# Second attention layer of a fused transformer kernel: from one token tile to pairs of token tiles, with every product but the keys' and values' as split fp32r products

## The reference

```python
sim = jnp.einsum('hid,hjd->hij', qh, kh) * SCALE          # 128 ** -0.5
mean = jnp.mean(sim, axis=-1, keepdims=True)
sim = (sim - mean) * ATTN_MATRIX_SCALE + mean             # 1.5
attn = jax.nn.softmax(sim, axis=-1)
out = jnp.einsum('hij,hjd->hid', attn, vh)                # then @ Wout + bout
```

## Time and profile before

| | us |
|---|---|
| median of 3 runs | 1071.01 (1070.51 to 1073.47) |
| span of the profiled execution | 1066.7 |
| PE busy in the span | 989.8 (93%) |
| DVE, POOL, ACT busy | 552.8, 429.3, 399.9 |
| experts end, L1's keys begin on PE | 637.0 |
| first output product of L1 starts | 697.08 |
| last output product of L1 starts | 951.72 |

### The profile page before, as it was taken

The page is one execution under the profiler, slowest core; times in us unless marked ns, Lnnn a source line. Parts: engine busy times, 40 slices in busy tenths (PEclk is TensorE's granted clock), DMA queues, the critical chain, the costliest instruction groups (busy, mean ns, idle before and its releaser), DMA issues.

```text
span 1066.7 us, 19273 instructions
## 1 busy us (share of the span) xinstructions
PE 989.8 (93%) x6204; PEld 809.6 (76%) x6205; DVE 552.8 (52%) x1349; ACT 399.9 (37%) x1340; POOL 429.3 (40%) x599
## 2 busy tenths in 40 slices
PE   5999999999997749999999998899999999999995
PEld 3599999999996625555555555899999999985662
DVE  7645454445544642222222226767676777653363
ACT  0255555554542202222222222444443434335442
POOL 5343334343332024433443336746565544331242
PEclk9999999999999569999999999999999999999887
DMA  9600000000000843111111114100000000000002
GB/s 298 248 2 1 1 0 1 2 2 1 0 1 1 308 141 98 40 48 40 39 41 47 39 34 135 42 11 20 10 20 10 21 1 2 2 1 1 1 1 79
DMA packets 29016, 47.71 MB, mean 45 GB/s; under 512 B 4493, under 2 KB 23105, under 8 KB 28705
## 3 DMA queue, kind: packets, MB, share of 16 engines
q1 hardware_dynamic: 25553, 37.68, 10.4%
q0 software_dynamic: 3408, 9.31, 3.2%
HBM read 37.68 MB, written 9.31 MB: 44 GB/s over the span
## 4 chain that ended last, share of the span: by engine, by line
PE 87%; DVE 7%; issue 2%; POOL 1%; DMA 1%; ACT 1%; POOLq 0%; SPq 0%; DVEq 0%; ACTq 0%
PE banks L428 16%; PE banks L1087 12%; PE banks L413 11%; PE banks L1126 7%; PE banks L420 6%; PE banks L399 6%; PE banks L390 6%; PE banks L391 5%; PE banks L392 5%; PE banks L340 2%; PE banks L1297 2%; PE banks L1112 2%; PE banks L1301 1%; PE banks L925 1%; DMA region_b<-xn_rows,token_now 1%
## 5 line engine op out<-in xcount | busy, mean ns | idle before, releaser
L859 POOL TENSOR_TENSOR region_a<-region_a,recip 128x512 f32<-128x512 f32 x128 | 133.2, 1041 | 294.9 <-DVE recip L648 294.7
L428 PE MATMUL banks<-region_a 128*128 128x128 f32 x1536 | 193.0, 275 | 1.9 <-DVE oT_low L668 1.7
L428 PEld LDWEIGHTS banks<-region_a 128*128 128x128 f32 x1536 | 181.8, 192 | 3.4 <-issue 2.6
L1087 PE MATMUL banks<-W,region_b 128*128 x312 | 149.6, 603 | 0.6 <-ACT region_b L1134 0.6
L413 PE MATMUL banks<-xT,region_b 128*128 128x128 f32 x1024 | 129.9, 282 | 3.2 <-DVE q_low L589 1.4
L773 ACT ACTIVATE region_a<-banks,negmax 128x154 f32<-128x154 f32 x256 | 96.0, 388 | 90.8 <-DVE negmax L632 88.3
L413 PEld LDWEIGHTS banks<-xT,region_b 128*128 128x128 f32 x1024 | 124.0, 198 | 4.5 <-DVE q_low L589 1.8
L1173 DVE TENSOR_TENSOR region_b<-banks,region_a 128x512 f32<-128x512 f32 x78 | 54.0, 692 | 114.8 <-PE banks L1087 114.8
L1221 POOL TENSOR_TENSOR region_b<-region_b 128x512 f32<-128x512 f32 x39 | 49.3, 1264 | 146.5 <-DVE region_b L1173 144.4
L773 ACT ACTIVATE region_a<-banks,bias 128x308 f32<-128x308 f32 x128 | 65.0, 513 | 110.9 <-DVE bias L644 110.9
L668 DVE TENSOR_TENSOR oT_low<-banks,oT_high 128x256 fp32r<-128x256 f32 x128 | 54.3, 424 | 91.5 <-ACT oT_high L764 91.5
(11 more groups left out here) (207 smaller groups left out, 1760.7 us busy)
## 6 DMA issues: line engine op xcount, KB each, us to landing
W<-in_L_ffn_W SPq DMA_DIRECT2D x1, 8192.0 KB, 27.4
y_slots<-region_b SPq DMA_DIRECT2D x39, 128.0 KB, 1.7
region_a<-in_L_ffn_b SPq DMA_DIRECT2D x1, 4096.0 KB, 18.7
region_a<-in_L_ffn_W SPq DMA_DIRECT2D x1, 4096.0 KB, 29.8
region_b<-in_L_xattn_Wq SPq DMA_DIRECT2D x2, 1024.0 KB, 8.3
xn_rows<-region_b SPq DMA_DIRECT2D x1, 2048.0 KB, 9.4
out<-x SPq DMA_DIRECT2D x4, 512.0 KB, 3.0
region_b<-in_L_xattn_Wk SPq DMA_DIRECT2D x2, 768.0 KB, 6.1
```

The lines of the kernel that those rows point to most:

```text
L428: mm = pe.matmul(o_ps[:, u * P:(u + 1) * P], V[:, b, 2 * g + u, i, :], probsT[:, g % 2, m * P:(m + 1) * P], start=(i == 0), stop=(i == 2))
L859: pool.tensor_tensor(whole, pr[:, :, 0:split], rc.broadcast_to([P, L.hs, split]), ALU.mult)
L1087: mm = pe.matmul(banks[:, 2 * r + part, :], xgT[:, r, k, :], w, start=(k == 0), stop=(k == DK - 1))
```

## The change

L1 gets functions of its own: `pe_pairs`, `dve_pairs`, `act_pairs` and `pool_pairs`. The unit is a pair of token tiles; a body has 8 steps n, of head group n // 2 and tile n % 2, and 4 groups. Layer 0, the experts and the coupling keep their work. The keys are multiplied with a context that is already shifted by a third of its mean, so the additional score column and the two small DVE operations go. In the loop:

- q, scores, PV and output are all split fp32r products: q 12 per group, scores 6 per step (308 columns), PV 18 per group, output 24 per tile; q and PV have 256 moving columns (both tiles). Weights and V are split ahead (`Wq_high`, `Wq_low`, `V_high`, `V_low`).
- Probabilities are normalised in place by one POOL instruction of 640 columns; ACT takes the high part of all 640 transposed columns, DVE the rest. Both happen in every step. High part and rest of q and o are of 512 columns, four times per pair each.
- In each step PE issues the transposes of the step before, and then the scores of the next one.

```diff
+                for n in range(8):
+                    s = 8 * i + n
+                    if not (first and n == 0):
+                        pe.wait_ge(sem("p_norm"), s0 + s)
+                        if not (first and n == 1):
+                            pe.wait_ge(sem("pt2_low"), s - 1)
+                        pe_pair_probsT(pe, (n - 1) % 8)
+                    if not (last and n == 7):
+                        if n % 2 == 1:
+                            pe.wait_ge(sem("q2_sb"), 4 * i + (n + 1) // 2 + 1)
+                        if not (first and n == 0):
+                            pe.wait_ge(sem("p_exp"), s0 + s)
+                        pe_pair_scores(pe, (n + 1) % 8)
...
+                    if n == 1 and not first:
+                        pe.wait_ge(sem("q2_sb"), 4 * i + 3)
+                        pe_pair_q(pe, 3)
+                    if n == 2 and not first:
...
+                        pe_pair_out(pe, 0, misc_ps, 4 * i)
+                    if n == 3 and not first:
+                        pe.wait_ge(sem("y_done"), t0 + 2 * i - 1)
+                        pe_pair_out(pe, 1, misc_ps, 4 * i)
+                    if n == 4 and not last:
...
+                        pe_pair_x(pe)
+                    if n == 5 and not last:
+                        pe.wait_ge(sem("xt2_sb"), i + 2)
+                        pe_pair_q(pe, 0)
+                    if n == 6 and not last:
+                        pe.wait_ge(sem("q2_sb"), 4 * i + 5)
+                        pe_pair_q(pe, 1)
+                    if n % 2 == 1 and not (first and n == 1):
...
+                        pe_pair_pv(pe, (n // 2 - 1) % 4)
+                    if n == 7 and not last:
+                        pe.wait_ge(sem("q2_sb"), 4 * i + 6)
+                        pe_pair_q(pe, 2)
```

DVE's body (`dve_pairs`), with the waits inside its helpers left out; `probsT_rest`, `pair_q_rest`, `pair_x_rest` and `o_rest` each wait for ACT's high part:

```diff
+                for n in range(8):
...
+                    reciprocals(n, s)
+                    if not (last and n == 7):
+                        row_max((n + 1) % 8, s + 1)
+                    if not (first and n == 0):
+                        probsT_rest((n - 1) % 8, s - 1)
...
+                    if n == 1 and not first:
+                        pair_q_rest(4 * i + 4, 3)
+                    if n in (2, 3) and not first:
+                        add_y(dve, L1, 2 * i + n - 4, n - 2, misc_ps[:, 0:D])
+                    if n == 4 and not last:
+                        pair_x_rest(i + 2)
+                    if n > 4 and not last:
+                        pair_q_rest(4 * i + n, n - 5)
+                    if n % 2 == 1 and not (first and n == 1):
+                        o_rest((n // 2 - 1) % 4, 4 * i + n // 2 - 1)
```

ACT's body and the POOL work that stands in the first one:

```diff
+                        probsT_high((n - 1) % 8, s - 1)
+                    if not (last and n == 7):
+                        exponentials((n + 1) % 8, s + 1)
...
+                    if n == 4 and not last:
+                        x_high(i + 2)
+                    if n in (5, 6) and not last:
+                        pair_q_high(4 * i + n, n - 5)
+                    if n % 2 == 1 and not (first and n == 1):
+                        o_high((n // 2 - 1) % 4, 4 * i + n // 2 - 1)
+                    if n == 7 and not last:
+                        pair_q_high(4 * i + n, n - 5)
...
+                    pool.tensor_tensor(probs1[:, n % 2], probs1[:, n % 2], rc, ALU.mult).then_inc(sem("p_norm"), 1)
+                    if first and n in (1, 2):
+
+                        pool.wait_ge(sem("Wo_high"), 2)
...
+                        pool.tensor_tensor(Wo_low[:, part], Wo1[:, part], Wo_high[:, part].bitcast(F32),
```

Ahead of the loop PE makes the values first, then the keys, and each unit is evacuated twice (ACT high, DVE rest). Then DVE normalises two tiles, ACT casts Wq (2048 columns), DVE makes its rest, and the first q group follows. Behind the loop come the last group's PV between two early coupling stages, and both outputs one after the other:

```diff
+            pe_pair_probsT(pe, 7)
+            pe_stage(pe, *EARLY[0], 0)
...
+            pe_pair_pv(pe, 3)
+            pe_stage(pe, *EARLY[1], 0)
...
+            pe_pair_out(pe, 0, misc_ps, GROUPS)
+            pe_pair_out(pe, 1, o_ps, GROUPS)
```

More of the change, by code:

```diff
@@ L341, in pe_kv, with dve_kv @@
                 mm.then_inc(sem("kv_ps"), 1)
[L343 to L346, removed]
+        def dve_kv(dve, L, kinds):
+            for n, (kind, a, half) in enumerate(kv_units()):
+                if kind not in kinds:
                     continue
-                dve.wait_ge(sem("kv_ps"), base + n + 1)
+                dve.wait_ge(sem("kv_ps"), n + 1)
                 bank = kv_bank(n)
-                if kind == "k" and L.index == 0:
+                if kind == "k":
                     for i in range(2):
@@ new lines, in remainder_rows, with act_kv1 @@
+        def remainder_rows(j):
+            return slice(64 * j, 64 * j + 64)
+        def act_kv1(act, L, kinds):
+            for n, (kind, a, half) in enumerate(KV1_UNITS):
+                if kind not in kinds:
+                    continue
+                act.wait_ge(sem("kv1_ps"), n + 1)
+                bank = kv1_bank(n)
+                if kind == "k":
+                    last = act.activation(K_high[:, a, :], bank[:, 0:KEYS], ACT.Copy, scale=L.scale)
+                elif kind == "v":
+                    last = act.copy(V_high[:, half * 4:half * 4 + 4, a, :], bank.rearrange("p (c n) -> p c n", c=4))
+                else:
+                    act.wait_ge(sem("v_zero"), 1)
+                    for j in range(2):
+                        rows = remainder_rows(j)
+                        last = act.copy(V_high[rows, half * 4 + j:half * 4 + 4:2, 2, :],
+                                        bank[rows, :].rearrange("p (g j n) -> p g j n", g=2, j=2)[:, :, j, :])
+                last.then_inc(sem("kv1_high"), 1)
@@ L386, in bodies, with pair_bodies @@
                         emit(i, False, False, before, batch, after)
+        def pair_bodies(eng, L, emit):
+            for first, end, peeled in L.bodies:
+                if peeled:
+                    emit(first, first == 0, end == PAIRS)
+                else:
+                    with eng.Fori(first, end) as i:
+                        emit(i, False, False)
         def pe_split(pe, o, left, right, start, stop):
@@ new lines, in pe_pair_scores, with pe_pair_probsT @@
+        def pe_pair_scores(pe, n):
+            g, rows = n // 2, slice(n % 2 * P, (n % 2 + 1) * P)
+            for u in range(2):
+                c = 2 * g + u
+                mm = pe_split(pe, scores[:, n % 2, u, 0:KEYS], (q_high[:, c, rows], q_low[:, c, rows]),
+                              (K_high[:, c, :], K_low[:, c, :]), True, True)
+            mm.then_inc(sem("s_ps"), 1)
+        def pe_pair_probsT(pe, n):
+            for m in range(5):
+                mm = pe.transpose(probsT_ps[:, m * P:(m + 1) * P], probs_row[:, n % 2, m * P:(m + 1) * P], ident[:])
+            mm.then_inc(sem("pt_ps"), 1)
@@ L572, in dve_attention @@
         def dve_attention(dve, L):
[L573 to L590 removed]
+            dve.wait_ge(sem("x_first"), 16)
```

839 lines of the change are left out of this document (518 added, 321 removed).

## The result

The change makes the kernel slower: median 1095.36 us of 4 runs (1092.50 to 1096.44) against 1072.24 us of 4 runs before (1070.51 to 1073.59), ratio 1.0204 (95% interval 1.0180 to 1.0227), +23.1 us. The span of the profiled execution is 1093.3 against 1066.7, +26.6.

The account below looks back on a forecast made before the run. PE alone was taken to bound L1's loop. Slower pairs 5.4, the two ends 1.4 and clock falls 7.7 summed to +14.5 us: span 1081.2, median 1085 with 4.3 above the span; range 1064 to 1097.

Parts of the forecast that it names:

- the likeliest case: Whole kernel: slower pairs, costlier ends and clock falls in five of seven bodies; 1085 us, own range 1079 to 1091.
- rival 3: Loop: clock falls twice per body, or gaps lengthen and step 2's wait appears; 1096 us, chance 0.15.
- PE's work: L1's loop: PE's work per pair drops from 35.3 to 32.2 us, saving 3.0 us if PE alone counted.
- The waits: L1's loop: PE waits 4.0 us per pair, mainly steps 0 and 4; pair 36.2 against 35.24, 5.4 for six pairs.
- The upper bound's 0.3 for waits on a register: Hardware loop: 0.3 more on the waits for a register, bringing them to 5.0 us per pair.
- The clock: Step 0's hole lowers PE's clock in five of seven bodies, 1.5 us each: +7.7 us.
- Its sign, a clock in L1 below 0.97: Profile of the changed kernel: the forecast is right if the clock in L1 is below 0.97.
- The stretch ahead of the loop: Before L1's loop: first transposes of probabilities come at 671.2, where they are now too (671.60).
- First and last body and the end: First body ends at 699.6, last output at about 961.4 against 954.6; both ends, head included, cost 1.4 us.
- the clock that holds (1): Loop: holes too short to lower PE's clock; +6.8 us, 1078 us, chance 0.22.
- That the chain is shorter (2): Steps 0, 4 and 6: DVE's chain behind `o_rest` is shorter, so faster; 1064 us, floor about 1050, chance 0.23.
- Rival 4: Split products: fp32r products of 256 columns cost as much as fp32; called excluded, given no chance.

Follow-up runs that it names:

- Run 10: Changed kernel with PE issuing scores before transposes, o's rest of step 7 put off, x's high part and rest moved earlier: 1064.46 us, ratio 0.9914.
- run 1: Changed kernel with 16 unread products of 256 columns filling PE's hole in step 0: 1085.33 us, ratio 1.0114 to the kernel before.
- run 9: Changed kernel with DVE's mixing of tiles 0 and 1 moved behind the keys' rests: 1093.49 us, ratio 1.0187 to the kernel before.
- run 3: Changed kernel with DVE taking the probabilities' rest ahead of the row maximum and o's rest one step later: 1092.04 us, ratio 1.0152.
- run 2: Changed kernel with only PE's order as before, scores ahead of transposes: 1075.35 us in 10 runs, ratio 1.0001 to the kernel before.
- run 4: Changed kernel, PE's order kept; DVE takes probabilities' rest before row maximum, reciprocals and x's rest earlier; ACT takes x's high part earlier: 1078.78 us, ratio 1.0076.
- run 6: Changed kernel with run 2's PE order, run 4's DVE and ACT orders, mixing behind the keys and Wo's split later: 1091.51 us, ratio 1.0180.

## Why the prediction was right, and where its size was off

The sign held and the range held narrowly (1064 to 1097; measured 1095.4). The forecast of 1085 was 10 us low, and the measured time lies outside the 1079 to 1091 given for the likeliest case, at the price of rival 3 (1096), though not by its two falls per body. The sum was +14.5 against +23.1. By its steps:

- **PE's work.** Right. PV's 18 products take 2.2 us (the group from 965.22 to 967.44), q's 12 take 1.4 (857.06 to 858.48), the scores 0.94. Run 10 needs 33.4 with 1.2 of holes: 32.2, the figure predicted.
- **The waits.** Right in place, releaser and size: 2.19 before the transposes of step 1 (predicted 2.3) and 1.2 before those of step 5 (1.3), from one start of transposes to the next 3.75 us (3.8), and 3.6 to 3.8 us of waits in a body (4.0). The upper bound's 0.3 for waits on a register in the hardware loop is shown by no run: the same waits are 1.19 and 0.20 in its bodies and 1.28 and 0.29 in the unrolled ones. Without the clock the pair is 36.1 (run 1), predicted 36.2; for six pairs +5.2 against 5.4 (36.2 - 35.24 would have made it 5.8).
- **The clock.** Right in its price, 1.5, and nearly right in its count: five falls were taken for seven bodies, and it fell in six. It fell once more where no fall was counted, in the last PV group, where 18 products take 3.7 us (971.23 to 974.95) instead of 2.2. Seven times 1.5 are 10.5 us, where 7.7 was taken. The reasoning left out a row that bears on it: the kernel before has a longer hole, the 3.18 at 670.47, and behind it the granted clock is 0.50 from 672 to 674 us. Its sign, a clock in L1 below 0.97, came out on the edge: 0.97.
- **The stretch ahead of the loop.** This is the step that failed: "first transposes at 671.2, where they are now too". They come at 681.08, of which 3.7 belongs to L1's later start, so the term is +5.8 and not -0.4. The prediction put DVE's work in a row but let PE's keys flow past it. The trace shows that the keys wait 3.87 for DVE's evacuation, which stands behind the mixing, and with 11.8 us of waits instead of 6.8 the clock falls twice in this stretch instead of once. The first transposes of x came at 664.52, where 656.1 had been placed.
- **First and last body and the end.** 3.4 measured, less 1.5 for the clock in the last PV group: 1.9, against 1.8 predicted.

The differences -0.2, +2.8, +6.2 and +0.1 make 8.9; the forecast was low by 23.1 - 14.5 = 8.6. So the stretch ahead of the loop is most of the miss.

Of the rivals, the clock that holds (1) is run 1: there the time is 1085, not 1078, the difference being the head again. That the chain is shorter (2) is refuted by the timeline. Of rival 3 ("falls twice per body") one half came true: one fall in six of seven bodies, none behind the hole of 1.2. In the chances, the parts of rivals 1 and 2 that end within 0.3% add up to 0.10 and not to the 0.12 given. Rival 4 is excluded as argued: an fp32r product of 256 columns costs 0.12 here as well. What no step of the prediction asked was whether the waits could be had away by an order, and that is what the runs show: PE's order alone is worth 2.9 us per pair, more than the 2.4 that the change lost.

## What to carry to other kernels

An engine that works in order answers in the order of its own list: when a producer's issue order is turned, turn the lists of all who read it (here DVE and ACT), or leave it. Either order was about equally good with matched readers (34.7 and 34.8 per pair, or 17.6 and 17.8 to 18.0 per tile), and a mismatch cost 1.5 to 4 us more per pair, falls of the clock included. When a hole has been found, ask of each reader what stands ahead of the late operation in its queue, not how long that operation takes. And a stretch ahead of a loop, in which each operation runs once, must be laid out for every engine at once, since it cost here 5.8 us, more than two of the pairs lost together.

## What the runs showed of the hardware

- A hole of PE of 2.19 us lowered the granted clock in six of the seven bodies of the changed kernel that have it, with PE fully busy on either side; one of 2.21 behind the loop did the same (0.58 from 971.0 to 974.9). The Trainium skill, TensorE: Matmul & The Clock Gate, "HAM oscillation — how this bites in real kernels", describes a loop in which every iteration's wait sends PE back to the slow clock; the trace of the changed kernel agrees in these six bodies, with 0.80 and 0.77 in the two slices at step 0 of one of them.
- The hole's length alone does not settle it. Behind the earliest hole of 2.19 the clock stayed at 1.00, and in run 1 so it did behind a hole of 2.21 in front of the last PV group (961.4 to 965.1). In run 9 one of six pairs with the same hole of 2.19 lasted 36.1 us, as without a fall, and in run 3 one of six pairs with a hole of 1.82 lasted 37.6, as with one. In runs 2, 4 and 10 the clock stayed at 1.00 over 200 us, with holes of up to 1.97. A shorter hole can lower it: in run 6 three of six pairs lasted 37.8 to 37.9, and the clock fell in them not behind the hole of 1.73 to 1.75 before step 1's transposes but behind one of 1.25 to 1.26 before step 5's q, which has another of 0.36 shortly ahead of it. What else decides is not shown. One of the three in run 6's timeline, and the window behind it:

```profile
768.51 0.39 PE L477 MATMUL banks<-xT_high,Wq_high 128*128 128x256 f32 x1 [1.26 <-DVE xT_low L902]
768.50:772.00 3.50, 3.49 (x19) 3.49 (x20) 2.45 (x6) 1.90 (x6) 2.84 (x3) 0.62 0.04 8
```

- The fall costs 1.5 us of path although the engine is slow for some 3.6 us (862.23 to 865.79), and is paid on top of the hole that caused it. Filling the hole with products that nobody reads bought 10 us (1095.4 to 1085.3), about half of what the right order of PE bought (20 us, to 1075.4).
